# Router logits taken as eight more columns of the two projections, with the rank products and residual sums put in another order

## What is computed

```python
h = _rmsnorm(x, ln1_w)
qkv = jnp.einsum('bsh,oh->bso', h, wqkv)
...
x = x + jnp.einsum('bso,ho->bsh', attn, wo)
h = _rmsnorm(x, ln2_w).reshape(-1, HID)
logits = jnp.einsum('th,eh->te', h, gate_w)
rprobs = jax.nn.softmax(logits.astype(jnp.float32), axis=-1)
topw, topi = jax.lax.top_k(rprobs, TOPK)
...
for e in range(E):
    g = jax.nn.silu(h @ w1.T) * (h @ w3.T)
    out = out + jnp.einsum('tf,hf->th', g, w2[e]) * wfull[:, e:e + 1]
return x + out.reshape(B, S, HID)
```

## Time and profile before

| | |
|---|---|
| median of 3 runs | 1732.0 us (1731.3 to 1738.56) |
| the profiled execution's own time | 1730.77 us |
| its span, first to last instruction | 1729.1 us |
| stage 7, from its first instruction to the first product of the experts | 1212.6 to 1345.5 us |
| busy in the span: PE, DVE, ACT, POOL | 94%, 67%, 54%, 32% |
| mean granted clock of PE | 0.97 of full speed |

### The profile page before, as it was taken

One profiled execution on the slowest core, in us unless ns is written; L12 is line 12 of the kernel. 1 busy time (PEld: TensorE's weight loads), 2 busy tenths in 40 slices (PEclk: granted clock), 3 DMA queues, 4 the chain that ended last, 5 costly groups with the idle time before them and its releaser, 6 DMA issues. The chain is left out here.

```text
span 1729.1 us, 29571 instructions
## 1 busy us (share of the span) xinstructions
PE 1624.7 (94%) x9040; PEld 807.7 (47%) x9040; DVE 1166.1 (67%) x3195; ACT 931.3 (54%) x2069; POOL 556.0 (32%) x842
## 2 busy tenths in 40 slices
PE   7899989899999999999999999998995899999996
PEld 3367655333333333334333343332884455565554
DVE  6722788899888888888888888870685344343342
ACT  6134544166676776676676766667573333333332
POOL 3530338163515003030030300000377344444443
PEclk9999999799999999999999999999895899999999
DMA  5000000311030300303003030000378677777774
GB/s 165 1 7 19 2 1 7 62 36 28 2 62 2 62 2 1 62 2 62 2 1 62 2 62 2 1 1 1 120 234 276 122 129 130 131 130 129 129 126 71
DMA packets 252195, 105.77 MB, mean 61 GB/s; under 512 B 208064, under 2 KB 247880, under 8 KB 252040
## 3 DMA queue, kind: packets, MB, share of 16 engines
q1 hardware_dynamic: 233296, 80.62, 22.0%
q0 software_dynamic: 13392, 18.49, 6.3%
q10 hardware_dynamic: 5352, 4.76, 0.8%
HBM read 30.88 MB, written 23.67 MB: 32 GB/s over the span
## 5 line engine op out<-in xcount | busy, mean ns | idle before, releaser
L1677 ACT ACTIVATE prob<-pS 128x512 f32<-128x512 f32 (+3 forms) x1280 | 582.3, 542 | 267.5 <-PE pS L1563 176.2
L1734 DVE TENSOR_REDUCE mx<-pM 128x1 f32<-128x512 f32 x768 | 501.6, 685 | 71.3 <-PE pM L1543 68.1
L1543 PE MATMUL pM<-KT,QT 96*128 96x512 bf16 (+3 forms) x1280 | 434.1, 356 | 16.5 <-DVE mx L1734 5.5
L1559 PE MATMUL pS<-QT,KT 99*128 99x512 bf16 (+3 forms) x1280 | 422.9, 352 | 6.8 <-ACT prob L1677 1.8
L2440 PE MATMUL bank<-w13T,QKV 128*128 x568 | 257.2, 596 | 15.4 <-ACT QKV L2467 15.4
L1730 DVE CUSTOM_DVE_ANT_0 junk<-pM,mask_row 128x128 bf16<-128x128 f32 (+3 forms) x512 | 239.9, 483 | 41.7 <-PE pM L1543 41.1
L1578 PE MATMUL pO<-prob,VV 128*32 128x512 f32 (+3 forms) x2560 | 267.8, 536 | 0.0
L1543 PEld LDWEIGHTS pM<-KT,QT 96*128 96x128 bf16 x1280 | 124.5, 98 | 208.5 <-DVE mx L1734 79.1
L1468 POOL CAST mpart<-mneg 128x16 bf16<-128x16 f32 x32 | 6.8, 213 | 653.9 <-DVE mneg L1742 653.9
L1559 PEld LDWEIGHTS pS<-QT,KT 99*128 99x128 bf16 x1280 | 123.6, 97 | 184.0 <-ACT prob L1677 140.2
L2500 DVE TENSOR_TENSOR QKV<-QKV,bank 128x512 f32<-128x512 f32 x71 | 48.8, 687 | 235.5 <-issue 200.2
(11 more groups left out here) (356 smaller groups left out, 1947.3 us busy)
## 6 DMA issues: line engine op xcount, KB each, us to landing
raw<-in_ffn_w_dram SPq DMA_DIRECT2D x48, 256.0 KB, 4.0
QKV<-queue SPq DMA_DIRECT2D x71, 136.0 KB, 2.5
out_dram<-x ACTq DMA_DIRECT2D x8, 512.0 KB, 4.7
x<-_attn_hidden_states_dram SPq DMA_DIRECT2D x14, 256.0 KB, 5.5
QKV<-QKV SPq DMA_TRANSPOSE x142, 3.2
QT<-mrow SPq DMA_DIRECT2D x128, 3.0 KB
out_dram<-QKV POOLq DMA_INDIRECT x71, 3.9
wc_s<-in_attn_Wc_dram SPq DMA_DIRECT2D x1, 1024.0 KB, 8.1
```

The costliest lines, as they stand in the source:

```text
L1543: last = nc.tensor.matmul(pM[:, bank, 0:w], QT[0:ROWS, par, h, qt * P:(qt + 1) * P], KT[0:ROWS, par, 512 * part:512 * part + w], start=Tru ...
L1559: last = nc.tensor.matmul(pS[:, p % NSC, lo:512], KT[0:ROWS + 3, par, kt * P:(kt + 1) * P], QT[0:ROWS + 3, par, h, 512 * c + lo:512 * c + ...
L1677: nc.scalar.activation(prob[:, n % RING, h, lo:512], pS[:, p % NSC, lo:512], ACT.Exp, scale=SCALE).then_inc(s.head_exp, 1)
L1734: nc.vector.reduce_max(mx[:, h, qt, part:part + 1], pM[:, plan.bank[item], 0:w], AX.X).then_inc(s.unit_max, 1)
```

## The change

The gate's rows are scaled by the second norm's weight in stage 4, turned as one more piece, and put beside `wqkv` as 8 further columns; a product of the turned gate with `wo` gives 8 further columns beside `wo`. So the projection of stage 6 gives for each tile 392 columns in place of 384, and that of stage 7 264 in place of 256, and the sum of the two parts on DVE (`attended`, now over 264 columns) holds the logits. `turn_h`, `logits` and `h_out` fall away. A new `routed` on DVE scales the first part, one small instruction a group. POOL gets two small multiplications in stage 6.

Stage 7 has 10 beats. `soften`, `records` and `choose` treat group b-1 (before: b-2) and stand after `settle`; `attended` is first in a beat; `ranks` of group b-2 stand near the head of PE's beat (before: near its end). The experts' weights start one beat earlier, and ACT does `squares` of group b and the next group's `normal` at the end of a beat. `pX` has three banks of one tile each, and a product waits for the sum three tiles back. Small buffers move; the load of the second norm's weight moves from the start of stage 6 to that of stage 7.

```diff
-        wqkvT = sb("wqkvT", [P, C, QKVW])
+        wqkvT = sb("wqkvT", [P, C, QKVW + E])
...
+                def output_gate():
+                    pe.wait_ge(s.wT_out, 6)
+                    for m in range(C):
+                        for c in range(C):
+                            last = nc.tensor.matmul(pQK[:, 1, m * E:(m + 1) * E], raw[:, 3 + c, m * P:(m + 1) * P],
+                                                    v.gws[:, c, :], start=(c == 0), stop=(c == C - 1))
                     last.then_inc(s.wT_mm, 1)
...
-                    if FIRST <= t < FIRST + 6:
+                    if FIRST <= t < FIRST + 7:
                         turn_weight(t - FIRST)
+                    if t == FIRST + 7:
+                        output_gate()
...
-    LATE = NQ + 3
+    LATE = NQ + 2
...
-            per = [0, 0, 4, 4, 4, 4, 4, 4, 8, 8, 8]
+            per = [0, 4, 4, 4, 4, 4, 4, 8, 8, 8]
...
-            for beat in range(1, LATE):
-                if beat >= 3:
-                    scatter(beat - 3, 0, 4)
-                if beat <= NQ:
-                    root2(beat - 1)
-                if beat >= 3:
-                    scatter(beat - 3, 4, 4)
+            for beat in range(LATE):
+                if beat >= 2:
+                    scatter(beat - 2, 0, 4)
+                if beat < NQ:
+                    root2(beat)
+                if beat >= 2:
+                    scatter(beat - 2, 4, 4)
...
                     if beat < NQ:
                         turn_attended(2 * beat + j)
-                    if 1 <= beat <= NQ:
-                        turn_h(2 * (beat - 1) + j)
+                    if j == 0 and beat == NQ + 1:
+                        total()
+                    if j == 0 and beat >= 2:
+                        ranks(beat - 2)
                     turn_weights(ws[j * quarter:(j + 1) * quarter])
                 for j in range(2):
                     if beat < NQ:
                         project(2 * beat + j)
-                    if 1 <= beat <= NQ:
-                        logits(2 * (beat - 1) + j)
                     if j == 0:
                         turn_weights(ws[2 * quarter:3 * quarter])
-                if beat == NQ + 1:
-                    total()
-                if 2 <= beat <= NQ + 1:
-                    ranks(beat - 2)
                 turn_weights(ws[3 * quarter:])
...
+                if beat < NQ:
+                    attended_out(2 * beat)
+                if beat == 0:
+                    normal(0)
+                weights_out(ws[0:quarter])
+                if beat < NQ:
+                    attended_out(2 * beat + 1)
+                weights_out(ws[quarter:2 * quarter])
+                if beat < NQ:
+                    squares(beat)
                 if 1 <= beat <= NQ:
-                    squares(beat - 1)
+                    exponential(beat - 1)
                 weights_out(ws[2 * quarter:3 * quarter])
+                if beat + 1 < NQ:
+                    normal(beat + 1)
...
+            def routed(q):
+                four = slice(G * q, G * q + G)
+                if q >= 1:
+                    dve.wait_ge(s.x2, G * q)
+                nc.vector.tensor_tensor(xl[:, :, H:H + E], QKV[:, four, ROUTED:ROUTED + E], bc(v.norm1[:, 0, four]),
+                                        ALU.mult).then_inc(s.routed, 1)
...
             for beat in range(LATE):
-                if 2 <= beat <= NQ + 1:
-                    soften(beat - 2)
-                    records(beat - 2)
-                    choose(beat - 2)
-                if beat == 4:
+                if beat == 3:
                     spare_out()
                 if beat < NQ:
                     attended(beat)
-                if 2 <= beat <= NQ + 1:
+                if beat + 1 < NQ:
+                    routed(beat + 1)
+                if beat >= 2:
                     settle(beat - 2)
                 if beat == 2:
                     spare_hot()
+                if 1 <= beat <= NQ:
+                    soften(beat - 1)
+                    records(beat - 1)
+                    choose(beat - 1)
                 if beat < NQ:
                     residual(beat)
```

More of the change, by code:

```diff
@@ L1106, in stages_layer2 @@
     with ExitStack() as late:
-        ln2_b = sb("ln2_b", [P, H], F32, late)
-        woT, gwT = v.woT, v.gwT
+        woT = v.woT
         mv5 = sb("mv5", [P, T, 2], F32, late)
@@ L1815, in stage7 @@
         turned = sb("turned7", [P, E * REC], F32, ctx)
-        aT, hT = (turned[:, 4 * C * P * n:4 * C * P * (n + 1)].rearrange("p (i j c n) -> p i j c n", i=2, j=2, c=C)
-                  for n in range(2))
+        aT = turned[:, 0:4 * C * P].rearrange("p (i j c n) -> p i j c n", i=2, j=2, c=C)
         padr = turned[:, :].rearrange("p (e w) -> p e w", e=E)
-        ln2c = sb("ln2c", [P, C], F32, ctx)
-        gws = sb("gws", [P, C, E], F32, ctx)
         raw = sb("raw8", [P, R, 512], F32, ctx)
@@ L1953, in project @@
                 pe.wait_ge(s.aT_out, i + 1)
-                if i >= 2:
-                    pe.wait_ge(s.x2, 2 * i - 2)
                 for j in range(2):
+                    t = 2 * i + j
+                    if t >= SX:
+                        pe.wait_ge(s.x2, t - SX + 1)
                     for c in range(C):
-                        last = nc.tensor.matmul(pX[:, 2 * (i % 2) + j, :], aT[:, i % 2, j, c, :], v.woT[:, c, :],
+                        last = nc.tensor.matmul(pX[:, t % SX, :], aT[:, i % 2, j, c, :], v.woT[:, c, :],
                                                 start=(c == 0), stop=(c == C - 1))
                     last.then_inc(s.proj, 1)
-            def turn_h(i):
-                pe.wait_ge(s.x2, 2 * i + 2)
-                if i >= 1:
-                    pe.wait_ge(s.hT_out, i)
-                for j in range(2):
-                    for c in range(C):
-                        last = nc.tensor.transpose(pH[:, j, c, :], QKV[:, 2 * i + j, c * P:(c + 1) * P],
-                                                   ident[:, :])
-                last.then_inc(s.hT_mm, 1)
-            def logits(i):
-                if i == 0:
-                    pe.wait_ge(s.gw_ready, C)
-                pe.wait_ge(s.hT_out, i + 1)
-                q = i // 2
-                if i % 2 == 0 and q >= 1:
-                    pe.wait_ge(s.soft, 2 * (q - 1) + 1)
-                if i % 2 == 0 and q >= 2:
-                    pe.wait_ge(s.place, q - 1)
-                for j in range(2):
-                    for c in range(C):
-                        last = nc.tensor.matmul(logits_at[:, 2 * (i % 2) + j, :], hT[:, i % 2, j, c, :], gws[:, c, :],
-                                                start=(c == 0), stop=(c == C - 1))
-                last.then_inc(s.logits, 1)
             def ranks(q):
@@ L2055, in attended_out @@
                 nc.scalar.copy(aT[:, i % 2], pA[:, :, :, :]).then_inc(s.aT_out, 1)
-            def h_out(i):
-                act.wait_ge(s.hT_mm, i + 1)
-                if i >= 2:
-                    act.wait_ge(s.logits, i - 1)
-                nc.scalar.copy(hT[:, i % 2], pH[:, :, :, :]).then_inc(s.hT_out, 1)
             def normal(q):
@@ L2100, in route_act @@
                 quarter = len(ws) // 4
-                if beat == NQ + 1:
+                if beat == NQ:
                     act.wait_ge(s.proj, T)
-                    act.wait_ge(s.logits, T // 2)
                     nc.scalar.activation(turned[:, :], ones[:, 0:1].to_broadcast([P, E * REC]), ACT.Copy,
                                          scale=0.0).then_inc(s.pad_zero, 1)
-                for j in range(2):
-                    if beat < NQ:
-                        attended_out(2 * beat + j)
-                    if 1 <= beat <= NQ:
-                        h_out(2 * (beat - 1) + j)
-                    weights_out(ws[j * quarter:(j + 1) * quarter])
-                    if j == 0 and 2 <= beat <= NQ + 1:
-                        exponential(beat - 2)
-                    if j == 0 and beat < NQ:
-                        normal(beat)
+                if beat < NQ:
[8 more added lines that the diff above has]
+                    squares(beat)
                 if 1 <= beat <= NQ:
-                    squares(beat - 1)
+                    exponential(beat - 1)
                 weights_out(ws[2 * quarter:3 * quarter])
+                if beat + 1 < NQ:
+                    normal(beat + 1)
                 if beat == LATE - 1:
@@ L2150, in soften @@
                 dve.wait_ge(s.rstd2, q + 1)
[L2151 removed]
+                dve.wait_ge(s.x2, G * q + G)
                 if q >= 1:
                     dve.wait_ge(s.ex, q)
[L2154 removed]
+                nc.vector.tensor_tensor(lg[:, :, :], QKV[:, four, H:H + E], bc(rstd[:, 4, four]), ALU.mult).then_inc(s.soft, 1)
                 dve.wait_ge(s.soft, 2 * q + 1)
@@ L2235, in route_dve @@
             nc.vector.memset(prior[:, 0, :], 0.0).then_inc(s.prior0, 1)
-            dve.wait_ge(s.ln_in, 16)
-            for c in range(C):
```

(9 more changed lines are left out.)

99 lines of the change are left out of this document (59 added, 40 removed).

## The result

The changed kernel takes 1761.08 us (median of 4 runs, 1757.55 to 1765.49) against 1734.37 (1731.3 to 1738.56) for the kernel before, run beside it: 1.015 times as long, 95% interval 1.013 to 1.0171. It is slower, as forecast, by 27 us and not by 36. The profiled execution took 1762.8 us, its span is 1761.1, and PE's mean granted clock fell from 0.97 to 0.955.

What follows compares the result with a forecast made beforehand. POOL's scatters end stage 7, and PE and DVE waiting on each other by turns each beat would delay them: 1730.8 + 36.6 (group 5 scattered late) + 0.4 (stage 4) = 1767.8, forecast 1768 us, range 1740 to 1788.

Steps and rivals of the forecast that it cites:

- The 31 and 10.7 us behind: End of stage 7: 31.04 us from group 5's first scatter to the last, then 10.7 to the first expert product, both unchanged.
- POOL hides the ring: Rival for stage 7: PE and DVE's alternation fits within POOL's 12 us a beat, both `squares` stalls go; 1726 us, chance 0.15.
- PE's leg: Stage 7, each beat: PE's ranks, weights, turn and two projections while DVE waits; 10.0 us, 6.3 at the higher clock throughout.
- DVE's leg: Stage 7, each beat: DVE's last sum, `routed`, `settle`, `soften`, `records` and `choose` to the last prior while PE waits; 6.96 us.
- Half clock through the first projection, full after it: Clock case forecast for PE's work after each wait in stage 7: 10.0 us, a beat of 17.0; chance 0.5.
- Full clock: Rival for stage 7: PE stays fast despite its waits, beats of 13.3 us, scatters 10.7 late; 1742 us, chance 0.15.
- 19.4: Rival for stage 7: PE at half clock throughout, beats of 19.4 us, group 5 53.8 late; 1785 us, chance 0.2.
- The start: Start of stage 7: PE waits some 4 us for ACT's third copy; first scatter at 1251.3 against 1237.80.
- To group 5: Stage 7: five rounds of 17.0, plus 2.6 for `spare_hot` and 2.2 for eight weight pieces; group 5's scatters 36.6 us late.
- Elsewhere: Outside stage 7: 0.4 us for stage 4's extra piece and products, 0 for stage 6's wider columns, bound 0.9.
- The signs: Expected in stage 7's profile: PE idle 4 to 6 us before ranks, POOL waiting for `settle`, DVE idle before third and fourth sums.

## Why the prediction was right, and where it was not

- **What bounds stage 7, and the direction.** Right: POOL's scatters set the end, and POOL waits for `settle` in each group up to the fifth. The 31 and 10.7 us behind came as 31.18 and 10.5. The rival on the other side (POOL hides the ring) needed PE's leg to be under 5.0 us; it is 7.7 and more.
- **DVE's leg: 6.96.** From the start of the last sum to the ranks are 6.91 us (1301.41 to 1308.32).
- **PE's leg: 10.0. This is the term that was mis-sized.** From the ranks at 1293.57 to the last sum at 1301.41 are 7.84 us; in rounds of 15.9 it is 8.9 to 9.0. "Half clock through the first projection, full after it" took the earlier trace rows, where PE restarted with a projection of 3.68 us. Here the ranks, two pieces and a turn come first and take the slow stretch or most of it, and the projection behind them takes 2.04 (at 1297.01), 3.12 or 3.19 against the 3.80 reckoned. Rounds of 14.6 to 15.9 stand against 17.0. Full clock was measured as 13.0 with PE kept busy, a little under the 13.3 reckoned, and no round reached 19.4.
- **The start.** The third copy made PE wait 3.92 us (some 4 forecast), and its turn came 11.9 us into the stage (12.1 forecast). The first scatter came 3.6 us sooner than forecast, counted from the start of the stage (35.1 against 38.7), by the same reckoning of the clock: 1.6 us up to the sums of group 1, 2.1 in the leg behind the ranks.
- **To group 5.** 79.5 us from the first scatter against the 89.1 of the forecast. With the 3.6 that is 13.2 of the 36.6 us. `spare_hot` shows (the first round takes 17.2); the 2.2 for eight pieces does not (the last takes 15.87; there the pieces took the slow stretch and the projection ran at 1.95). The sum let 0.2 us pass between `settle` and the scatter of group 5 where it had 0.9 at the start; 0.8 was measured.
- **Elsewhere.** Stage 4 took 0.4 more, as reckoned. Width was costed at 0 in stage 6, and the median of the run with width alone bears that out. 5.8 + 2.1 + 0.4 us of the profiled execution come from stretches outside stages 4 and 7: 37.0 - 13.2 + 8.3 = 32.1, against 32.0 measured. They are no part of the mechanism, and they may be why the profiled spans differ by more than the medians (26.7). That the profiled span came so near to the forecast is luck to that extent: stage 7 grew by 23.3 us and not by 36.6, and 8.3 us from elsewhere stand beside it.
- **The signs.** PE's wait before the ranks and POOL's for `settle` came as named. DVE's did not: of the few us before the third and fourth sum, 0.90 and 0.46 came, and its wait for PE (2.53 in the round above, 3.34 in those of 15.83 and 15.90) stands before the first sum.
- **What the prediction did not see.** It put ACT's order into the start alone. In every beat ACT's copy also stood behind the squares, and so behind DVE's last sum: a ring of 13.3 to 13.5 us (with the ranks moved back), its copy ready 1.2 us ahead of the ranks. It cost the forecast nothing, since the slower ring counts, but whoever had repaired the kernel by the prediction would have won 4.5 of 23 us.
- **The clock.** The ranks start each round at 0.60 to 0.61 us where they take 0.30 to 0.39 at the higher level, after every wait of 5.4 to 6.2. So the clock's price comes back in each round: 14.6 to 15.9 against 13.0. The Trainium skill (TensorE: Matmul & The Clock Gate, section "HAM oscillation — how this bites in real kernels") tells of such a loop with 1.67 us at the low clock in each pass. This trace agrees on the return in each pass and has more of it: the slow rows run from 1293.57 to 1297.01 in the round shown, and on into the projection in those of 15.83 and 15.90.

## What to carry to other kernels

When a product is moved to the head of an engine's list, look for each wait in that list that leads back to the engine's own output through others: such a round, and not the sum of the work, is then the pace. Look behind it for the next ring that is nearly as long (here ACT's copy, ready 1.2 us before the wait ended), since undoing one of the two shows little (here 4.5 and 0.0 us of the 21.9 that both gave) and would acquit a true cause. Read such a run where the ring ends, here at the first scatter of group 5, and not only at the end of the stage, where a moved product can cost something else. A pass of waits can also cost the clock behind each wait, and that price is best read from a restart with the same first instructions.

## What was not expected of the hardware

- PE stood 1.80 us before the ranks with PE kept busy and went on at the higher clock in two rounds (ranks 0.38, projection 1.95); in the round before, after the same 1.80 us, its pieces took 1.09, and in the round behind a turn took 1.06. In the kernel before, the projection took 3.68 after a wait of 1.58 and 1.99 after one of 1.46, a third wait that the prediction leaves out. The length of a wait alone did not tell what the clock does.
- Executions of the same code differ by up to 4 us ahead of stage 4 (156.2 to 160.2 among the variants), and a wait of PE there is 4.39 us in some and 6.54 in others.
